# Causal attention with its probabilities built with keys on partitions: maxima from a separate pass, shift and sums as products with ones, two heads on the halves of the array

## The chip, the cores and the metric

The kernel runs on 1 core of one Trainium2 chip. The metric is device time in microseconds (us). The kernel before takes 1363.31 us, the median of 3 runs (1360.38 to 1364.28).

## The reference

The program is four layers on `x` of shape (1, 2048, 128): causal softmax attention with 16 heads of 64, a gated feed-forward layer, a linear attention, and the feed-forward layer again. Only the first is changed:

```python
K = jnp.einsum('bpd,ihd->biph', x, W_K)
Q = jnp.einsum('bpd,ihd->biph', x, W_Q)
V = jnp.einsum('bpd,ihd->biph', x, W_V)
scores = jnp.einsum('biph,biqh->biqp', K, Q)
scores = jnp.where(mask[None, None, :, :], scores, NEG_INF)
attn = jax.nn.softmax(scores / np.sqrt(d_head).astype(np.float32), axis=-1)
z = jnp.einsum('biph,biqp->biqh', V, attn)
out = jnp.einsum('bqf,df->bqd', z_flat, W_O)
```

`x` in it is the normalised input, and `out` is added to the residual. Everything is fp32.

## The kernel before, in words

`attention` (L192) handles the 16 heads as 8 pairs. The 2048 positions are 16 tiles of 128, and 4 chunks of 512. A pair's steps `j` = 0 to 7 are two tiles of queries each, so a step has four rows of work `u` (2 tiles by 2 heads). For each row and each chunk of keys up to the diagonal:

- **Scores** (L516 to L519). Queries stand on the partitions. Q is split into a rounded part and a remainder (`q_hi`, `q_lo`), K likewise, and K's two parts of 64 rows are stacked into 128 (`k_st`), so two matmuls over all 128 rows give all four products. Matmuls of type fp32r are used. At the diagonal a bf16 matmul adds the mask (L518). The scores lie in a ring of 5 PSUM banks.
- **Softmax.** VectorE takes the negated maximum of each row and chunk (L353); ScalarE computes the exponentials into `prob` in SBUF with this as bias, and sums them along the way (L434, with an ACTIVATION_READ_ACCUMULATOR for the sum). Small instructions (L306 to L369) combine chunks, and each piece of `prob` is multiplied by its factor: three in four on GpSimd (L325), one in four on VectorE (L382).
- **Turning.** The value product needs keys on partitions, so each 128x128 block of `prob` is transposed by TensorE (L530) and copied to `probT` by ScalarE (L448) for one head and VectorE (L376) for the other.
- **Values** (L545): fp32 matmuls with 64 columns of V as weights, each head to its own half of the output partitions; then a copy (L455), the output projection (L555) and the addition to `x` (L391).

Each pair's K and Q come from L561, V from L568. ScalarE writes the rounded parts (L464, L466), VectorE the remainders (L408, L410), and SP copies `q_parts` to the other 64 partitions by DMA (L287). fp32 matmuls show in the trace as two records of two streams each.

The order of every engine's work is made by `attention_plan` (L51), a list scheduler over assumed durations; it emits one list per engine. Each engine then runs its list in order, and waits on semaphores. `fetch` (L1211) loads the feed-forward weights and clears its scratch rows; SP issues it once the first pair's projections are through.

## Time and profile before

| | |
|---|---|
| median of 3 runs | 1363.31 us |
| profiled execution | 1360.53 us, span 1358.8 us |
| mean granted TensorE clock | 0.944 |
| PE busy | 1173.5 us, 86% |
| DVE, ACT, POOL busy | 957.3, 794.6, 829.2 us |
| attention, from the page's stretches and the timeline | up to about 1018 us |

The profile's page gives busy time per engine and a strip of 40 equal slices; the trace gives windows, groups of instructions by line, the waits and a timeline. PE is the matmul row, PEld the row of weight loads, DVE is VectorE, ACT ScalarE, POOL GpSimd. The duration of a matmul record includes the time until its result has left the array, so what a matmul costs in a stream is read from one start to the next. All times below are of the one profiled execution.

### The profile page before, as it was taken

The page shows a single profiled execution, that of the slowest core. Times are in us where ns is not written, and L with a number is a line of the kernel's source. Part 1 is how long each engine was busy: PE and PEld are TensorE (multiplying, and loading weights), DVE is VectorE, ACT ScalarE, POOL GpSimd, SP SyncE. Part 2 cuts the span into 40 slices and gives each one's busy share as a digit, 9 for nine tenths or more (in the row PEclk, how much of TensorE's full clock was granted, in tenths as well). Part 3 has the DMA queues.
Part 4 walks back from the last instruction along what each step waited for, and adds up shares of the span by engine and source line. Part 5 has one row for each costly group of instructions (what it writes and reads, how often), then busy time and mean ns, then how long its engine had stood idle before and what let it go on. Part 6 is the DMA issues. An engine that isn't in the chain of part 4 may idle for free. (4 is left out here: it accounts for less than half of the span.)

```text
span 1358.8 us, 24424 instructions
## 1 busy us (share of the span) xinstructions
PE 1173.5 (86%) x7936; PEld 855.3 (63%) x7936; DVE 957.3 (70%) x2108; ACT 794.6 (58%) x2192; POOL 829.2 (61%) x813
## 2 busy tenths in 40 slices
PE   5999999999999999999999999999973585885285
PEld 4666667676767767676676667676753582443285
DVE  5878677867776786878677777867743355998254
ACT  6777576767757775766677576766721342322053
POOL 0675668757866775887576768757852443552433
PEclk9899999999999999999999999999995796998588
DMA  4950200200020011002000200200000221000023
GB/s 124 125 141 16 48 1 1 52 12 1 1 63 1 1 32 32 1 1 63 1 1 8 57 1 1 50 14 1 1 1 17 57 61 32 1 0 1 29 60 98
DMA packets 52689, 41.18 MB, mean 30 GB/s; under 512 B 14177, under 2 KB 41442, under 8 KB 52578
## 3 DMA queue, kind: packets, MB, share of 16 engines
q1 hardware_dynamic: 50018, 34.50, 11.9%
q0 software_dynamic: 2560, 5.26, 1.2%
q8 instruction: 62, 1.02, 0.3%
q14 instruction: 49, 0.40, 0.1%
HBM read 13.49 MB, written 9.48 MB: 17 GB/s over the span
## 5 line engine op out<-in xcount | busy, mean ns | idle before, releaser
L325 POOL TENSOR_SCALAR at_prob<-at_prob,at_scale 128x512 f32<-128x512 f32 (+1 forms) x480 | 656.2, 1383 | 5.6
L353 DVE TENSOR_REDUCE at_nmax<-at_ps 128x1 f32<-128x512 f32 (+3 forms) x640 | 375.9, 603 | 154.1 <-PE at_ps L519 150.5
L434 ACT ACTIVATE at_prob<-at_ps,at_nmax 128x512 f32<-128x512 f32 (+3 forms) x640 | 393.1, 623 | 44.6 <-DVE at_nmax L353 43.7
L530 PE MATMUL at_ps<-ident,at_prob 128*128 128x128 f32 x2176 | 328.7, 275 | 23.4 <-DVE at_probT L376 19.1
L530 PEld LDWEIGHTS at_ps<-ident,at_prob 128*128 128x128 f32 x2176 | 255.7, 140 | 110.5 <-issue 52.6
L516 PE MATMUL at_ps<-at_k_st,at_q_parts 128*128 128x512 f32 (+3 forms) x640 | 285.1, 445 | 6.1 <-ACT at_prob L434 3.6
L448 ACT ACTIVATE at_probT<-at_ps 128x512 f32<-128x512 f32 (+1 forms) x288 | 165.1, 573 | 212.2 <-PE at_ps L530 188.0
L545 PE MATMUL at_ps<-at_probT,at_v 128*64 128x256 f32 (+1 forms) x2304 | 270.1, 374 | 12.3 <-DVE at_probT L376 12.3
L519 PE MATMUL at_ps<-at_k_st,at_q_parts 128*128 128x512 f32 (+3 forms) x640 | 253.1, 396 | 0.0
L376 DVE COPY at_probT<-at_ps 128x512 f32<-128x512 f32 (+1 forms) x288 | 189.0, 656 | 68.1 <-PE at_ps L530 64.7
L545 PEld LDWEIGHTS at_ps<-at_probT,at_v 128*64 128x64 f32 x2304 | 155.2, 136 | 107.1 <-issue 48.5
L516 PEld LDWEIGHTS at_ps<-at_k_st,at_q_parts 128*128 128x128 f32 x640 | 122.2, 191 | 46.7 <-ACT at_prob L434 22.0
L434 ACT ACTIVATION_READ_ACCUMULATOR at_prob<-at_ps,at_nmax 128x1 f32 x640 | 131.1, 205 | 0.0
L519 PEld LDWEIGHTS at_ps<-at_k_st,at_q_parts 128*128 128x128 f32 x640 | 125.8, 197 | 1.3
L382 DVE TENSOR_SCALAR at_prob<-at_prob,at_scale 128x512 f32<-128x512 f32 (+1 forms) x160 | 93.0, 583 | 2.5 <-POOL at_scale L318 2.0
L727 POOL DMA_INDIRECT slots_out<-f_ys,f_back x48 | 47.2, 984 | 63.9 <-DVE f_ys L836 49.2
L866 ACT ACTIVATE f_hT<-f_ps,f_wfix 128x128 f32<-128x128 f32 x192 | 54.6, 370 | 34.1 <-PE f_ps L911 28.8
L306 POOL TENSOR_TENSOR at_gap<-at_low,at_nmax 128x8 f32<-128x8 f32 (+2 forms) x48 | 9.9, 206 | 93.8 <-DVE at_low L358 93.8
L720 POOL DMA_INDIRECT slots_in<-f_xn,f_pos_u x32 | 31.3, 980 | 55.7 <-DVE f_pos_u L811 46.6
L904 PE MATMUL f_ps<-ident,f_xs 128*128 128x128 f32 x48 | 14.2, 296 | 57.3 <-DMA f_xs<-slots_in 57.3
L1037 POOL TENSOR_TENSOR li_outer<-li_qk,li_v 128x1152 f32<-128x1152 f32 x16 | 35.5, 2220 | 44.1 <-DVE li_qk L1063 44.1
L316 POOL COPY at_scale<-at_rinv 128x4 f32<-128x4 f32 x16 | 3.0, 189 | 96.6 <-DVE at_rinv L364 96.6
(189 smaller groups left out, 1364.1 us busy)
## 6 DMA issues: line engine op xcount, KB each, us to landing
at_q_parts<-at_q_parts SPq DMA_DIRECT2D x64, 256.0 KB, 3.5
f_xs<-slots_in SPq DMA_DIRECT2D x48, 64.5 KB
slots_in<-zeros SPq DMA_DIRECT2D x2, 1536.0 KB, 19.4
wall<-in_L_ffn_w_dram SPq DMA_DIRECT2D x1, 2048.0 KB, 19.8
wall<-in_L_ffn_w_dram SPq DMA_DIRECT2D x4, 512.0 KB, 6.1
f_got<-slots_out SPq DMA_DIRECT2D x8, 256.0 KB, 3.6
out_dram<-x SPq DMA_DIRECT2D x4, 256.0 KB, 2.4
slots_out<-f_ys,f_back POOLq DMA_INDIRECT x48
```

The costliest lines, as they stand in the source:

```text
L325: pool.tensor_scalar(cols, cols, scale[:, k, u, c:c + 1], None, ALU.mult).then_inc(s_fix["pool"], 1)
L353: dve.tensor_reduce(nmax[:, j % 2, u % 4, c:c + 1], bank, AX.X, ALU.max, negate=True).then_inc(s_max, 1)
L376: dve.tensor_copy(probT[1][n % TURNED][:, 0:w], turn_ps[1][:, 0:w]).then_inc(s_probT[1], 1)
L382: dve.tensor_scalar(cols, cols, scale[:, k, u, c:c + 1], None, ALU.mult).then_inc(s_fix["dve"], 1)
L434: act.activation(prob[j % 2][u % 4][:, c * BANK:c * BANK + w], ring[use_of["score", p, u, c] % RING][:, 0:w], ACT.Exp, bias=nmax[:, j % 2, ...
L448: act.activation(probT[0][n % TURNED][:, 0:w], turn_ps[0][:, 0:w], ACT.Copy).then_inc(s_probT[0], 1)
L516: pe.matmul(bank[:, 0:w], q_hi[h][:, r * P:(r + 1) * P], keys, start=True, stop=False)
L519: pe.matmul(bank[:, 0:w], q_lo[h][:, r * P:(r + 1) * P], keys, start=False, stop=True).then_inc(s_score, 1)
L530: last = pe.transpose(turn_ps[h][:, b * P:(b + 1) * P], prob[j % 2][2 * i + h][:, t * P:(t + 1) * P], ident[:, :])
L545: last = pe.matmul(z_ps[part_of, to:to + w], v[:, t, part_of], probT[h][group(p, j, g) % TURNED][:, 2 * P * b:2 * P * b + w], start=t == 0 ...
L727: pool.indirect_dma_start(scratch_out[:, :], bass.IndirectOffsetOnAxis(ap=back[k][:, :], axis=0), ys[k][:, :], None).then_inc(s_store[k], 16)
L866: last = act.activation(hT[k][:, f, :], ps[2 + c % 2][:, f * P:(f + 1) * P], ACT.Gelu, bias=wfix[k][:, B1.start + f:B1.start + f + 1])
```

## The change

The softmax is computed in another layout. `attention_order` replaces `attention_plan`: a fixed order with constants instead of durations. Work now goes by chunks of 512 queries (4 per pair), and by tiles of 128 keys inside them (4, 8, 12 and 16 tiles). A pair has 40 such tiles, and 40 items of the separate maxima pass.

- **Maxima pass** (`peakscore`): for 128 queries and up to 512 keys, one product `q_hi` by `k_hi` per head over 64 rows; at the diagonal four matmuls add the mask. VectorE takes maxima over both heads at once (`max`), and the smallest negated one (`peak`), which matmuls with the identity turn into a row (`turn`), copied to `shift`.
- **Scores** (`score`): keys on partitions, 512 queries as columns. Four products per head over 64 rows, the heads on the upper and lower half of the array and in two banks, plus one matmul with ones that adds `shift`. At the diagonal only the columns that count are computed.
- ScalarE takes the exponential of both heads (up to 128x1024) straight into `probT`, without bias and sum. GpSimd zeroes the masked triangle (`select`).
- **Values** as before, per tile with up to 512 columns. The **sums** of the probabilities are matmuls with 32 columns of ones, on the quarters of the output partitions.
- **End of a chunk**: copies (`leave`), a matmul that spreads the sums (`spread`), a VectorE reciprocal of 128x512 (`share`), a GpSimd product (`divide`), then the output projection.
- The PSUM ring is 3 pairs of banks, shared by all items but the values. `probT` has 6 buffers. The copies by DMA are gone; `fetch` is issued when the setup's transposes are done. GpSimd prepares more constants, and the setup's transposes wait for them.

```diff
-RING = 5
-TURNED = 4
+WAITING = 6
+RUN = 2
+AHEAD = 20
...
+    RING = 3
...
-                for _, p, c in order["sp"]:
...
+                sp.wait_ge(s_setT, N_SET)
+                fetch(sp)
...
+                    if kind == "select":
...
+                        pool.affine_select(out=tile, in_=tile, compare_op=ALU.is_ge, fill=0.0, base=0,
+                                           pattern=[[0, 2], [1, P]], channel_multiplier=-1).then_inc(s_select, 1)
+                    else:
...
+                        pool.tensor_tensor(z_sb[g % 2][:, :], z_sb[g % 2][:, :], share[:, :], ALU.mult).then_inc(s_zn, 1)
...
+                        dve.tensor_reduce(nmax[:, g % 2, t, :, k], ring[use_of["peakscore", p, c, t, k] % RING][:, :, 0:w], AX.X, ALU.max,
+                                          negate=True).then_inc(s_max, 1)
...
+                        dve.reciprocal(share[:, :], ring[use_of["spread", p, c] % RING][:, 0, :]).then_inc(s_share, 1)
...
+                        act.activation(probT[n % WAITING][:, :, at:BANK], ring[use_of["score", p, c, t] % RING][:, :, at:BANK],
+                                       ACT.Exp).then_inc(s_exp, 1)
...
-                pe.wait_ge(s_const, 3)
+                pe.wait_ge(s_const, CONSTS)
...
+                        for h in range(2):
+                            last = pe.matmul(banks[:, h, 0:w], q_hi[p % 2][head(h), (TPC * c + t) * P:(TPC * c + t + 1) * P],
+                                             k_hi[p % 2][head(h), k * BANK:k * BANK + w], start=True, stop=k < c)
+                        if k == c:
+                            for i in range(2):
+                                for h in range(2):
+                                    last = pe.matmul(banks[:, h, w - P:w], pick[i][head(h), :], mask[i][head(h), :], start=False, stop=i == 1)
...
+                        for a, b in ((k_hi, q_hi), (k_hi, q_lo), (k_lo, q_hi), (k_lo, q_lo)):
+                            for h in range(2):
+                                pe.matmul(banks[:, h, at:BANK], a[p % 2][head(h), keys], b[p % 2][head(h), queries], start=a is k_hi and b is q_hi, stop=False)
+                        for h in range(2):
+                            last = pe.matmul(banks[:, h, at:BANK], onesr[head(h), :], shift[c][head(h), at:BANK], start=False, stop=True)
...
+                        for t in tiles:
+                            at = skipped(c, t)
+                            for h in range(2):
+                                r = h + 2 * (t % 2 if c else 0)
+                                last = pe.matmul(l_ps[32 * r:32 * r + 32, at:BANK], ones[:, :], probT[tile_no[p, c, t] % WAITING][:, h, at:BANK],
+                                                 start=t == 0 or (t == 1 and c > 0), stop=t >= TPC * (c + 1) - (2 if c else 1))
```

What TensorE runs in the middle of a pair before (scores by L516 and L519, transposes by L530, values by L545):

```order
L545 MATMUL at_ps<-at_probT,at_v 64x256 [waits at_s_probT0,at_s_probT1,at_s_zT,at_s_v]
L545 MATMUL at_ps<-at_probT,at_v 64x256 x7
L516 MATMUL at_ps<-at_k_st,at_q_parts 128x512 [waits at_s_exp]
L519 MATMUL at_ps<-at_k_st,at_q_parts 128x512
L530 MATMUL at_ps<-ident,at_prob 128x128 [waits at_s_probT1,at_s_fix_dve,at_s_fix_pool]
L530 MATMUL at_ps<-ident,at_prob 128x128 x3
L516 MATMUL at_ps<-at_k_st,at_q_parts 128x256 [waits at_s_exp]
L518 MATMUL at_ps<-at_maskb,at_identb 128x128
L519 MATMUL at_ps<-at_k_st,at_q_parts 128x256
L530 MATMUL at_ps<-ident,at_prob 128x128 [waits at_s_probT0,at_s_fix_pool]
L530 MATMUL at_ps<-ident,at_prob 128x128 x3
```

And in the middle of a pair after the change (L454 and L459 the maxima pass, L475 and L477 the scores and the shift, L491 the values, L497 the sums, L503 the spread of the sums, L507 the output projection; line numbers are the changed kernel's):

```order
L507 MATMUL at_ring<-at_wo,at_z_sb 128x128 [waits at_s_zn,at_s_exp]
L507 MATMUL at_ring<-at_wo,at_z_sb 128x128 x3
L503 MATMUL at_ring<-at_l_sb,at_gather 128x512 [waits at_s_l,at_s_max]
L491 MATMUL at_z<-at_probT,at_v 64x512 [waits at_s_z,at_s_v,at_s_exp]
L491 MATMUL at_z<-at_probT,at_v 64x512 x3
L497 MATMUL at_l<-at_probT,at_ones 32x512 x4
L454 MATMUL at_ring<-at_k_hi,at_q_hi 128x128 [waits at_s_hi,at_s_exp]
L454 MATMUL at_ring<-at_k_hi,at_q_hi 128x128
L459 MATMUL at_ring<-at_mask,at_pick 128x128 x4
L475 MATMUL at_ring<-at_q_hi,at_k_hi 128x512 [waits at_s_shift,at_s_lo,at_s_add]
L475 MATMUL at_ring<-at_q_hi,at_k_hi 128x512
L475 MATMUL at_ring<-at_q_lo,at_k_hi 128x512 x2
```

The transposes are gone, each tile of scores has ten matmuls (two behind each of five weights), and every item waits for the reader of the item three before it (`at_s_max`, `at_s_exp`, `at_s_add`) instead of five.

On VectorE the maxima of the next chunks stand behind the reciprocal and the remainders:

```order
L323 TENSOR_REDUCE at_nmax<-at_ring 128x2 [waits at_s_peakscore] x3
L336 TENSOR_TENSOR at_k_lo<-at_ring,at_k_hi 128x512 [waits at_s_hi]
L337 SCALAR_TENSOR_TENSOR at_q_lo<-at_ring,at_q_hi 128x512
L343 RECIPROCAL at_share<-at_ring 128x512 [waits at_s_zn,at_s_spread]
L323 TENSOR_REDUCE at_nmax<-at_ring 128x2 [waits at_s_peakscore] x4
L350 TENSOR_TENSOR x<-at_ring,x 128x512 [waits at_s_add,at_s_o]
```

The list before had a copy of transposed probabilities or a scaling between every two or three maxima; these are gone.

## Rows read from the trace of the kernel before

**Rows 1.** The page: busy time, and 40 slices of the span

```profile
PE 1173.5 (86%) x7936; PEld 855.3 (63%) x7936; DVE 957.3 (70%) x2108; ACT 794.6 (58%) x2192; POOL 829.2 (61%) x813
PE   5999999999999999999999999999973585885285
```

**Rows 2.** Two of four windows of one pair each: busy us (instructions), clock, DMA

```profile
140.00:262.00 122.00, 116.88 (x827) 84.41 (x824) 90.50 (x178) 83.64 (x227) 84.73 (x80) 1.00 0.07 16
...
506.00:628.00 122.00, 117.75 (x833) 85.36 (x832) 92.70 (x180) 84.93 (x231) 85.64 (x80) 1.00 0.08 18
```

**Rows 3.** Groups by line, shapes kept apart: busy, mean ns | idle before

```profile
L325 POOL TENSOR_SCALAR at_prob<-at_prob,at_scale 128x512 f32<-128x512 f32 x320 | 511.7, 1613 | 4.7
L434 ACT ACTIVATE at_prob<-at_ps,at_nmax 128x512 f32<-128x512 f32 x448 | 304.7, 687 | 22.7 <-DVE at_nmax L353 21.9
L353 DVE TENSOR_REDUCE at_nmax<-at_ps 128x1 f32<-128x512 f32 x448 | 299.4, 684 | 125.4 <-PE at_ps L519 123.6
...
L325 POOL TENSOR_SCALAR at_prob<-at_prob,at_scale 128x128 f32<-128x128 f32 x64 | 38.3, 599 | 0.1
...
L408 DVE TENSOR_TENSOR at_k_st<-at_ps,at_k_st 64x512 fp32r<-64x512 f32 x64 | 44.1, 689 | 8.5 <-ACT at_k_st L464 6.9
...
L464 ACT ACTIVATE at_k_st<-at_ps 64x512 fp32r<-64x512 f32 x64 | 37.7, 589 | 11.4 <-PE at_ps L561 10.9
...
L434 ACT ACTIVATE at_prob<-at_ps,at_nmax 128x128 f32<-128x128 f32 x64 | 23.5, 367 | 14.2 <-DVE at_nmax L353 14.1
...
L353 DVE TENSOR_REDUCE at_nmax<-at_ps 128x1 f32<-128x128 f32 x64 | 18.0, 282 | 13.7 <-PE at_ps L519 13.5
```

**Rows 4.** Timeline of PE, fp32r scores in a row, then four transposes

```profile
609.03 0.40 PE L516 MATMUL at_ps<-at_k_st,at_q_parts 128*128 128x512 f32 x1
609.27 0.40 PE L519 MATMUL at_ps<-at_k_st,at_q_parts 128*128 128x512 f32 x1
609.50 0.60 PE L530 MATMUL at_ps<-ident,at_prob 128*128 128x128 f32 x4
609.86 0.48 PE L516 MATMUL at_ps<-at_k_st,at_q_parts 128*128 128x512 f32 x1
```

**Rows 5.** Timeline of PE, a packed run of values, eight matmuls

```profile
1009.38 1.95 PE L545 MATMUL at_ps<-at_probT,at_v 128*64 128x256 f32 x16
1011.26 0.98 PE L530 MATMUL at_ps<-ident,at_prob 128*128 128x128 f32 x7
```

**Rows 6.** Timeline of PE, an unpacked fp32 projection, eight records of L568

```profile
26.34 1.02 PE L561 MATMUL at_ps<-at_xnT,at_wT_k 128*128 128x512 f32 x2
27.20 1.05 PE L568 MATMUL at_ps<-at_wT_v,at_xnT 128*128 128x128 f32 x8
28.10 0.59 PE L561 MATMUL at_ps<-at_xnT,at_wT_q 128*128 128x512 f32 x1
```

**Rows 7.** Timeline of PEld: loads of 128 columns, gate product (clock at half)

```profile
1029.68 1.83 PEld L890 LDWEIGHTS f_ps<-f_gate,f_xnT 128*128 128x128 f32 x8
```

**Rows 8.** Timeline of PE: a score of 128 columns with its mask

```profile
42.16 0.22 PE L516 MATMUL at_ps<-at_k_st,at_q_parts 128*128 128x128 f32 x1
42.23 0.23 PE L518 MATMUL at_ps<-at_maskb,at_identb 128*128 128x128 bf16 x1
42.26 0.31 PE L519 MATMUL at_ps<-at_k_st,at_q_parts 128*128 128x128 f32 x1
42.41 0.52 PE L530 MATMUL at_ps<-ident,at_prob 128*128 128x128 f32 x3
```

**Rows 9.** Groups: reciprocals of 4 and of 16 elements

```profile
L364 DVE RECIPROCAL at_rinv<-at_esum 128x4 f32<-128x4 f32 x16 | 2.7, 170 | 0.7 <-ACT at_prob L434 0.7
...
L1073 DVE RECIPROCAL li_den<-li_den 128x16 f32<-128x16 f32 x16 | 4.0, 252 | 0.6
```

**Rows 10.** Timeline: the setup's constants on POOL, first transposes

```profile
4.51 0.29 POOL L298 TENSOR_SCALAR_AFFINE_SELECT at_maskb<-at_maskb 128x128 bf16<-128x128 bf16 x1
...
11.54 4.58 PE L487 MATMUL at_ps<-ident,at_prob 128*128 128x128 f32 x24 [11.54 <-DMA at_prob<-in_L_attn_a_W_Q_dram]
```

More of the change, by code:

```diff
@@ L195, in attention @@
     SCALE = float(DH) ** -0.5
-    STEPS = NT // 2
-    order, row, chunks, width, turned, fixer, run_of = attention_plan(PAIRS, NT, NC, TPC)
-    uses = [it for it in order["pe"] if it[0] in ("score", "project", "vproject", "out")]
+    order, runs = attention_order(PAIRS, NC, TPC)
+    RING = 3
+    uses = [it for it in order["pe"] if it[0] != "value"]
     use_of = {it: n for n, it in enumerate(uses)}
@@ L207, in attention, with head, cols, skipped @@
             count_of[(e,) + it] = ran[it[0]]
-    def group(p, j, g):
-        return p * STEPS * (STEPS + 1) // 2 + j * (j + 1) // 2 + g
-    value_run = {}
-    for it in order["pe"]:
-        if it[0] == "value":
-            for g in run_of(it[2], it[3]):
-                value_run[group(it[1], it[2], g)] = count_of[("pe",) + it]
+    tile_no, run_of = {}, {}
+    for i, run in enumerate(runs):
+        for n, it in enumerate(run):
+            tile_no[it], run_of[it] = RUN * i + n, run[0]
+    tile_at = {n: it for it, n in tile_no.items()}
+    def head(h):
+        return slice(DH * h, DH * (h + 1))
+    def cols(c):
+        return slice(c * BANK, (c + 1) * BANK)
+    def skipped(c, t):
+        return max(t - TPC * c, 0) * P
     with ExitStack() as ctx:
@@ L258, in attention @@
+        mask = [sb(f"mask{i}", [P, P], F32R) for i in range(2)]
+        onesr = sb("onesr", [P, P], F32R)
+        ones = sb("ones", [P, 32])
+        gather = sb("gather", [P, P])
+        draft = [probT[0][:, 0, i * P:(i + 1) * P] for i in range(4)] + [probT[1][:, 0, i * P:(i + 1) * P] for i in range(3)]
         s_xin, s_win = sem("s_xin"), [sem(f"s_win{i}") for i in range(4)]
[L259 removed]
+        s_c0, s_draft, s_halves, s_const = sem("s_c0"), sem("s_draft"), sem("s_halves"), sem("s_const")
@@ L391, in _ @@
+                        rows = x[:, TPC * c:TPC * (c + 1), :]
+                        o = ring[use_of["out", p, c] % RING][:, 0, :]
                         dve.tensor_tensor(rows, o.rearrange("p (t d) -> p t d", d=D), rows, ALU.add).then_inc(s_add, 1)
                         if p == PAIRS - 1:
-                            dve.wait_ge(s_add, q + 1)
-                            for t in (2 * j, 2 * j + 1):
+                            dve.wait_ge(s_add, g + 1)
+                            for t in range(TPC * c, TPC * (c + 1)):
@@ L554, in _ @@
-                        for i in range(2):
-                            last = pe.matmul(ring[use_of[it] % RING][:, i * D:(i + 1) * D], zT[q % 2][:, i * P:(i + 1) * P], wo[:, p, :],
-                                             start=True, stop=True)
+                        pe.wait_ge(s_zn, g + 1)
+                        for t in range(TPC):
+                            last = pe.matmul(banks[:, 0, t * P:(t + 1) * P], z_sb[g % 2][:, t * P:(t + 1) * P], wo[:, p, :], start=True, stop=True)
                         last.then_inc(s_o, 1)
@@ L558, in _ @@
                     elif kind == "project":
-                        _, _, c, i = it
-                        free_bank(it)
-                        pe.matmul(ring[use_of[it] % RING][:, :], wT["kq"[i]][:, p, :], xnT[:, c * BANK:(c + 1) * BANK],
-                                  start=True, stop=True).then_inc(s_proj, 1)
+                        for i, n in enumerate("kq"):
+                            last = pe.matmul(banks[:, i, :], wT[n][:, p, :], xnT[:, cols(c)], start=True, stop=True)
+                        last.then_inc(s_proj, 1)
```

591 lines of the change are left out of this document (249 added, 342 removed).

## The prediction

> **What bounds the kernel now.** I read the page first. TensorE is busy for 86% of the span and at nine tenths or more in all slices from about 34 to 1000 us [rows 1]: attention is one long stretch in which TensorE is the bound, and what follows it is not touched. Then the windows of a pair. I chose 122 us, and two of the four windows have nearly the same counts [rows 2]: PE is busy 116.9 to 117.8 of 122 us at a granted clock of 1.00, VectorE 90 to 93, ScalarE and GpSimd about 85. So one pair costs 122 us, 8 pairs cost 976, and a change is worth what it does to TensorE's 122 us, unless it makes another engine later than that. VectorE's idle time of 123.6 us before the maxima is a wait for scores [rows 3], so it follows and does not lead.
>
> Then I looked for prices in a stream, from start to start. All durations are of one profiled execution, 1360.53 us, 0.2% under the median of 1363.31; the sum is made against 1360.5. One measurement of this kernel can tell 0.3%, some 4 us, from no change.
>
> - An fp32r matmul of 512 columns takes 0.24 and 0.23 us [rows 4]: 0.235.
> - An fp32 matmul of 512 columns on the whole array takes 0.86 us, and one of 128 columns 0.90/4 = 0.225 [rows 6].
> - Eight value matmuls of 256 columns, on alternating halves of the columns, take 1.88 us [rows 5]. Alone each would take 0.43, together 3.44. Two at a time give 1.72, and 0.16 us is left for going into and out of the tiled array: 0.08 per change of tiling. A packed pair of 512 columns costs 0.86.
> - Loads of 4-byte weights, 128 columns: at half the clock eight take 1.83 us, the last of them 0.33, so one starts each 0.214 us [rows 7], and 0.107 at the full clock. With scores of 128 columns, two such loads and one bf16 mask cover 0.25 us from L516 to the next transpose [rows 8], which agrees: short matmuls cost their loads.
>
> **The change, part by part, for one pair.** A full item counts as 512 columns; the causal triangle is 34 of these per head (28 full, and 4 each of 384, 256 and 128).
>
> (1) Removed: 272 transposes. Four start 0.36 us apart from the next score [rows 4], and delay its second half by about 0.1: near 0.11 each, 30 us. The copies, the scaling on GpSimd (1.61 us a piece, [rows 3]) and the chain of small instructions were beside TensorE; their loss gives nothing by itself. The scores (128 full-width slots for two heads, and the narrow ones) were some 33 us.
>
> (2) Scores. Two heads on the two halves, so ten matmuls are five slots if halves overlap. No row of before shows halves of the rows at work at once. Its cost lies between the packed slot, 0.86/4 = 0.215 per 512 fp32r columns (the value rows, halves of the columns), and the unpacked double, 0.47. I take the fp32r row, 0.235, and full overlap, since the nearest packed rows lose nothing. 28 full items: 28 x 5 x 0.235 = 32.9. The 12 narrow ones are bound by ten loads, 1.07 us each, 12.8 (five slots of 384 columns are only 0.88). Sum 45.7.
>
> The loads are where the trace is silent: it has none of 64 rows. It could be half as long or go on beside the other half's load, 0.054 effective, or be 0.107 one behind the other. I take 0.107, as in rows 7; at 0.054 narrow scores and masks would save 10 us a pair. The Trainium skill (TensorE: Matmul & The Clock Gate, LDWEIGHTS) says that a load's time is its columns and that fewer rows take as long; it speaks against the change, and by it the saving of 10 is out.
>
> (3) Maxima pass. 24 full items at 0.235 = 5.6. The 16 diagonal ones have six loads each (two products, four mask matmuls), 0.64 us, 10.3. Sum 15.9. Nothing of this existed before but 32 masks of 0.04 us [rows 8].
>
> (4) Values: 34 packed pairs x 0.86 = 29.2, before nearly the same.
>
> (5) Sums: 68 fp32 matmuls with 32 columns. The first chunk uses two quarters (2.5 slots x 0.86 = 2.2); the others have 31.5 slots on four quarters, 0.43 if four work at once, 13.5. Sum 15.7. If only two do, 29.2.
>
> (6) Per pair also: turning the maxima, 16 loads, 1.7; spreading the sums, 4 x 0.86 = 3.4. Projections (6.9), V (32 records of 0.112, 3.6) and output (3.6) stay, 14.1.
>
> (7) Changes of tiling: three for each of 20 runs of values and sums, two for each of 20 items that use the whole array: 100 x 0.08 = 8.0 (before some 40 x 0.08).
>
> Sum: 45.7 + 15.9 + 29.2 + 15.7 + 5.1 + 14.1 + 8.0 = 133.7 us of TensorE.
>
> (8) Waits. Other engines per pair, from rows 3: a maximum costs 0.684 at 512 columns and 1.05 ns per column more, so 1.22 at 1024; all maxima are 42, with remainders (8 x 0.69), additions and reciprocals some 66. A reciprocal goes from 170 to 252 ns for 12 elements more [rows 9], 6.8 ns each: 3.6 us for 512. Exponentials: 0.83 ns per column, 1.11 at 1024, 39 in all, ScalarE 54. GpSimd under 25. None reaches 134. But the ring is three deep. A projection's banks are held for two copies and two subtractions, 2 x 0.589 + 2 x 0.689 = 2.6 us [rows 3], while the two items behind it give 1.4 to 2.4; 4 of these and 4 spreads held for 3.6 us are each worth about 1 us. A score frees its banks after 1.11 us and handing over, against 1.4 us of a maximum and a score: about nothing to 0.2. Between 3 and 12 us a pair; I take 7 (before: 122 less 117.7 busy, 4.3).
>
> (9) Start. GpSimd makes some 27 constants before TensorE may start: 8 fills of about 0.2 and 5 selects of 0.29 [rows 10], two copies of 512 columns (1.61 each) and ten smaller ones (0.6, both by GpSimd's nearest rows [rows 3]), some 13 us from 3.6 us on. The transposes began at 11.54 [rows 10] and then waited for weights: +5 us. `fetch` moves ahead and the 64 copies by DMA vanish; attention reads none of `fetch`'s data and copies of later pairs were issued long before use: 0. The last chunk ends through copies, reciprocal, product and output, some 10 us, where before the last scalings and transposes ran with TensorE half idle: 0.
>
> A pair: 133.7 + 7 = 140.7 against 122, +18.7; eight pairs +150, and 5: **1360.5 + 155 = 1516 us**, 11% slower. The same prices give the kernel before 33 + 1.3 + 30 + 29.2 + 14.1 + 3.2 = 111 and 4.3 idle, 115 of its 122 us; the other 7 are small delays where kinds of matmuls meet. The new stream has fewer such places beyond those counted in (7), so I don't add them, but were they there again, it would be +56.
>
> **The rivals.**
> Packing pays less than full. If quarters work only two at a time: +13.5 x 8 = 108, 1624. Against it, the values lose nothing on two halves [rows 5]; there is no row for four. The Trainium skill (same page, Part 3) measured 3.07 times for four row tiles. As a mechanism here, with a loss like this, each half slot of scores and maxima would be 30% longer, (32.9 + 5.6) x 0.3 x 8 = +92, 1608.
>
> Halves of the rows don't overlap: scores double but stay over their loads, 28 x 10 x 0.235 = 65.8 and 12 narrow ones 16.3, +36; maxima +7; less waiting, -3: +40 a pair, 1836. Against it: halves of the columns do overlap. For it: no row.
>
> The readers are late: ring waits of 17 us a pair rather than 7, 1596. For it: three places rather than five, the 3.6 us reciprocal with four maxima behind it. Against: every other engine has half its time free.
>
> The other side: the parts of the array are fully independent, also in loading weights and in changing the tiling. Then narrow scores fall to 8.0 (-4.8), diagonal maxima by 5.1, tiling by 8.0, slots to 0.215 (-3.3): -21.2, a pair of 119.5, 1360.5 - 20 + 5 = 1346, and 1290 if the waits go too. It decides once a pair is under 121.4 us. Against it: 0.16 us around each run of values [rows 5].
>
> **How the numbers follow.** Forecast 0.51 (its own range 1455 to 1580, from slots of 0.215 to 0.235, waits of 3 to 12, and those 56); packing less than full 0.20; late readers 0.10; no overlap of halves 0.12; other side 0.07. The range 1440 to 1640 takes in the first three, 0.81. Faster by over 0.3%: 0.06; within 0.3%: 0.02, at the edge of the other side; slower 0.92.
>
> **What would show it.** Right: PE over 90% busy at clock 1.00, a score item of 512 columns starting its ten matmuls within 1.1 to 1.2 us, in pairs a tenth apart; diagonal maxima items at 0.64; four sums of 512 columns in 0.9 us; attention ending near 1173. Wrong: matmuls of the two heads one behind the other by 0.2 us, four sums in 1.7 us, PE idle before maxima or scores with VectorE or ScalarE named for over 15 us a pair, or narrow scores of 128 columns under 0.6 us.

## The result and the profile after

The changed kernel takes 1478.2 us (median of 4, 1477.4 to 1480.4) where the kernel before takes 1361.85 (median of 4): 1.0856 times as long, 95% interval 1.0832 to 1.0881. The profiled execution took 1480.4 us, its span is 1478.7. The forecast was 1516, its range 1440 to 1640: slower, as predicted, and 38 us less slow.

The page of the changed kernel, busy time and two lines of its slices:

```profile
PE 1290.6 (87%) x9024; PEld 739.9 (50%) x9024; DVE 724.9 (49%) x1148; ACT 501.8 (34%) x864; POOL 240.7 (16%) x359
...
PE   5899999999999999999999999999996295886376
...
PEclk9999999999999999999999999999998587899588
```

Against [rows 1], VectorE has lost 232 us of work, ScalarE 293 and GpSimd 589, and TensorE has gained 117. The stretch at nine tenths now lasts to about 1110 us instead of 1000: all the engines that were relieved had stood beside the one that got more to do.

The window of one pair, from its first projection to that of the next pair; the three before and behind are the same within 0.01 us (us and instructions of each engine, the granted clock last but two):

```profile
503.87:641.24 137.37, 132.27 (x970) 70.52 (x969) 64.14 (x61) 48.68 (x64) 11.66 (x20) 1.00 0.00 1
```

A pair takes 137.4 us where it took 122.4 (the same measure on the kernel before; [rows 2] used 122). 8 x 15.0 = 120 us, and the spans differ by 1478.7 - 1358.8 = 119.9: the pairs hold the whole loss, the start and the layers behind attention hold none.

Groups by line, shapes kept apart (busy, mean ns | idle before, and what ended it), for [rows 3] and [rows 9]:

```profile
L323 DVE TENSOR_REDUCE at_nmax<-at_ring 128x2 f32<-128x1024 f32 x224 | 272.7, 1225 | 351.0 <-PE at_ring L454 286.9 <-PE at_ring L459 64.0
...
L343 DVE RECIPROCAL at_share<-at_ring 128x512 f32<-128x512 f32 x32 | 107.4, 3357 | 65.7 <-PE at_ring L503 65.7
...
L475 PEld LDWEIGHTS at_ring<-at_q_lo,at_k_hi 64*128 64x128 f32 x640 | 60.6, 186 | 5.8
```

The maximum of 1024 columns takes 1.225 us (1.22 was worked out from its shorter forms), the exponential 1.03 (1.11), the reciprocal 3.36 (3.6). Nearly all idle time of VectorE and ScalarE in attention is a wait for PE.

### The profile page after: what moved, and what is told of

The parts are those of the page before. It is cut to its first block and busy times, and to the rows that moved or that the text cites. A ratio compares the mean times of both kernels' runs of the same rounds, so it can differ in the third digit from the quotient of the medians.

```text
span 1478.7 us, 23229 instructions
## 1 busy us (share of the span) xinstructions
PE 1290.6 (87%) x9024; PEld 739.9 (50%) x9024; DVE 724.9 (49%) x1148; ACT 501.8 (34%) x864; POOL 240.7 (16%) x359
## 5 line engine op out<-in xcount | busy, mean ns | idle before, releaser
L323 DVE TENSOR_REDUCE at_nmax<-at_ring 128x2 f32<-128x1024 f32 (+2 forms) x320 | 338.5, 1065 | 490.6 <-PE at_ring L454 286.9
L381 ACT ACTIVATE at_probT<-at_ring 128x1024 f32<-128x1024 f32 (+1 forms) x320 | 286.5, 897 | 649.7 <-PE at_ring L477 648.4
L491 PE MATMUL at_z<-at_probT,at_v 128*64 128x512 f32 (+3 forms) x1280 | 270.4, 543 | 0.0
L497 PE MATMUL at_l<-at_probT,at_ones 128*32 128x512 f32 (+3 forms) x1280 | 162.9, 540 | 0.0
L454 PE MATMUL at_ring<-at_k_hi,at_q_hi 64*128 64x512 f32 (+3 forms) x640 | 135.4, 422 | 7.8 <-DVE at_q_lo L337 4.0
L491 PEld LDWEIGHTS at_z<-at_probT,at_v 128*64 128x64 f32 x1280 | 77.8, 136 | 124.4 <-issue 98.0
L475 PE MATMUL at_ring<-at_q_hi,at_k_hi 64*128 64x512 f32 (+3 forms) x640 | 129.2, 400 | 7.8 <-DVE at_nmax L323 7.6
L454 PEld LDWEIGHTS at_ring<-at_k_hi,at_q_hi 64*128 64x128 f32 x640 | 59.8, 185 | 147.8 <-issue 119.4
L475 PE MATMUL at_ring<-at_q_lo,at_k_hi 64*128 64x512 f32 (+3 forms) x640 | 116.9, 362 | 0.0
L475 PE MATMUL at_ring<-at_q_hi,at_k_lo 64*128 64x512 f32 (+3 forms) x640 | 116.9, 361 | 0.0
L475 PE MATMUL at_ring<-at_q_lo,at_k_lo 64*128 64x512 f32 (+3 forms) x640 | 116.9, 361 | 0.0
L477 PE MATMUL at_ring<-at_shift,at_onesr 64*128 64x512 f32 (+3 forms) x640 | 116.5, 360 | 0.0
L497 PEld LDWEIGHTS at_l<-at_probT,at_ones 128*32 128x32 f32 x1280 | 28.7, 108 | 109.5 <-issue 107.9
L475 PEld LDWEIGHTS at_ring<-at_q_hi,at_k_hi 64*128 64x128 f32 x640 | 60.4, 185 | 35.2 <-DVE at_nmax L323 24.9
L477 PEld LDWEIGHTS at_ring<-at_shift,at_onesr 64*128 64x128 f32 x640 | 60.5, 185 | 9.7
L475 PEld LDWEIGHTS at_ring<-at_q_lo,at_k_lo 64*128 64x128 f32 x640 | 60.3, 185 | 9.8
L475 PEld LDWEIGHTS at_ring<-at_q_hi,at_k_lo 64*128 64x128 f32 x640 | 60.3, 185 | 9.7
L475 PEld LDWEIGHTS at_ring<-at_q_lo,at_k_hi 64*128 64x128 f32 x640 | 60.6, 186 | 5.8
```

The lines of the kernel that those rows point to most:

```text
L323: dve.tensor_reduce(nmax[:, g % 2, t, :, k], ring[use_of["peakscore", p, c, t, k] % RING][:, :, 0:w], AX.X, ALU.max, negate=True).then_inc ...
L381: act.activation(probT[n % WAITING][:, :, at:BANK], ring[use_of["score", p, c, t] % RING][:, :, at:BANK], ACT.Exp).then_inc(s_exp, 1)
L454: last = pe.matmul(banks[:, h, 0:w], q_hi[p % 2][head(h), (TPC * c + t) * P:(TPC * c + t + 1) * P], k_hi[p % 2][head(h), k * BANK:k * BANK ...
L475: pe.matmul(banks[:, h, at:BANK], a[p % 2][head(h), keys], b[p % 2][head(h), queries], start=a is k_hi and b is q_hi, stop=False)
L477: last = pe.matmul(banks[:, h, at:BANK], onesr[head(h), :], shift[c][head(h), at:BANK], start=False, stop=True)
L491: pe.matmul(z_ps[head(h), at:BANK], v[p % 2][:, t, head(h)], probT[tile_no[p, c, t] % WAITING][:, h, at:BANK], start=t == 0, stop=t == TPC ...
```

## Where the 137.4 us of a pair go

Timeline of PE in the changed kernel, a full diagonal item of the maxima pass, a full tile of scores, and the next item ("x2" are the two heads):

```profile
608.73 0.50 PE L454 MATMUL at_ring<-at_k_hi,at_q_hi 64*128 64x512 f32 x2
609.07 0.34 PE L459 MATMUL at_ring<-at_mask,at_pick 64*128 64x128 f32 x4
609.24 0.45 PE L475 MATMUL at_ring<-at_q_hi,at_k_hi 64*128 64x512 f32 x2
609.52 0.40 PE L475 MATMUL at_ring<-at_q_lo,at_k_hi 64*128 64x512 f32 x2
609.76 0.40 PE L475 MATMUL at_ring<-at_q_hi,at_k_lo 64*128 64x512 f32 x2
609.99 0.40 PE L475 MATMUL at_ring<-at_q_lo,at_k_lo 64*128 64x512 f32 x2
610.23 0.39 PE L477 MATMUL at_ring<-at_shift,at_onesr 64*128 64x512 f32 x2
610.45 0.40 PE L454 MATMUL at_ring<-at_k_hi,at_q_hi 64*128 64x512 f32 x2
```

Both heads together start a product each 0.23 us: the halves of the rows overlap in full. A full score item takes 1.21 us (1.1 to 1.2 predicted). The full diagonal maxima item takes 0.51, not 0.64, and the narrower ones 0.37 to 0.40. The reason stands in the view of the loads for the same moment:

```profile
609.18 0.19 PEld L475 LDWEIGHTS at_ring<-at_q_hi,at_k_hi 64*128 64x128 f32 x2
609.29 0.19 PEld L475 LDWEIGHTS at_ring<-at_q_lo,at_k_hi 64*128 64x128 f32 x2
```

Two loads, one for each half, start together (0.003 to 0.004 us apart in the records) and are over in 0.19; the next two follow 0.11 later. I had taken 0.107 for each, one behind the other. Narrow tiles of scores show it best (timeline of PE, a tile of 256 and one of 128 columns):

```profile
602.20 0.28 PE L475 MATMUL at_ring<-at_q_hi,at_k_hi 64*128 64x256 f32 x2
...
602.80 0.39 PE L454 MATMUL at_ring<-at_k_hi,at_q_hi 64*128 64x512 f32 x2
603.69 0.33 PE L475 MATMUL at_ring<-at_q_hi,at_k_hi 64*128 64x128 f32 x2 [0.50 <-DVE at_nmax L323]
603.85 0.27 PE L475 MATMUL at_ring<-at_q_lo,at_k_hi 64*128 64x128 f32 x2
...
604.19 0.28 PE L477 MATMUL at_ring<-at_shift,at_onesr 64*128 64x128 f32 x2
604.40 1.12 PE L503 MATMUL at_ring<-at_l_sb,at_gather 128*128 128x512 f32 x2
```

The five slots of the 256-column tile take 0.60 us, where 1.07 was predicted. Those of the 128-column tile take 0.71 here, with a wait in front and an fp32 matmul behind: the first slot 0.16, the last 0.21, and the three between 0.11 to 0.12 each. Over five pairs tiles of 128 columns take 0.60 to 0.71. And the values and sums (timeline of PE, one run of two key tiles):

```profile
1090.60 1.94 PE L491 MATMUL at_z<-at_probT,at_v 128*64 128x512 f32 x8
1092.46 1.07 PE L497 MATMUL at_l<-at_probT,at_ones 128*32 128x512 f32 x8
1093.46 0.50 PE L475 MATMUL at_ring<-at_q_hi,at_k_hi 64*128 64x512 f32 x2
```

Each fp32 matmul has two records, so x8 are four matmuls. Four values take 1.86 us, two at a time. Four sums take 1.00 us, four at a time. Changing over is in both: by the prices of the prediction the streams alone are 1.72 and 0.86. The first fp32r product behind such work takes 0.33 us instead of 0.23, as at 608.73 above (0.34).

From start to start over five pairs (251.6 to 938.5 us of the trace), the parts of a pair add up as follows; a run is the values and sums of two key tiles, 20 a pair. The predicted column gives each part its changes of tiling at the 0.08 of term 7.

| part of a pair | predicted | measured |
|---|---|---|
| scores with shift: 28 full, 4 of 384, 8 narrower | 45.7 | 42.4 |
| maxima pass (L454 12.1, L459 3.0) | 15.9 | 15.1 |
| values and sums (32.2 + 19.0) | 44.9 + 4.8 | 51.2 |
| turning, spread, projections, V, output | 19.2 + 3.2 | 22.6 |
| waits and changes behind scores | 7 | 6.1 |
| pair | 140.7 | 137.4 |

The scores are 28 x 1.20 + 4 x 0.97 + 8 x 0.61 from timelines, without what stands behind them. From their first start to the next item's they take 48.5 us a pair, and the row of waits and changes is what is left of that. PE's idle time alone is 137.37 - 132.27 = 5.1 us a pair.

The same count in the kernel before, in us a pair: scores with masks 44.5, transposes 32.0, values 32.4, projections, V and output 13.5, in all 122.4. So the transposes went, and the sums (19.0), the maxima pass (15.1), the spread (4.2), the turning (2.3) and a longer score part (+4.0) came.

The longest rows of PE's own waits in attention, in the changed kernel (us in total, times, longest):

```profile
PE at_ring L503 <- DVE at_q_lo L337: 19.0, 14, 1.4
...
PE at_ring L507 <- DVE at_q_lo L337: 9.7, 7, 1.4
PE at_ring L475 <- DVE at_nmax L323: 7.6, 15, 0.6
```

The first two are the projections' banks, held for two copies and two subtractions: with 4.0 us before the maxima they make 32.7 us, 4.1 a pair. The third is a wait for maxima, which term 8 did not name. The reciprocal, which it did, is not among them.

## The experiments

Each time is a median of 4 runs. The kernel before, timed beside them, took 1360.8, 1360.7, 1359.6 and 1360.3 us. Differences to the changed kernel are taken from ratios times 1360, and are uncertain by some 4 us.

| kernel | us | ratio to before, 95% | against the change |
|---|---|---|---|
| heads_apart | 1489.9 | 1.0938 (1.0920 to 1.0956) | +11 |
| two_quarters | 1584.1 | 1.1628 (1.1609 to 1.1648) | +105 |
| recip_copy | 1476.2 | 1.0843 (1.0825 to 1.0861) | -2 |
| no_mask | 1458.3 | 1.0725 (1.0707 to 1.0743) | -18 |
| no_swap | 1469.1 | 1.0808 (1.0786 to 1.0830) | -7 |
| run4 | 1601.6 | 1.1786 (1.1764 to 1.1809) | +126 |
| run4_copy | 1473.1 | 1.0835 (1.0812 to 1.0858) | -3 |
| joined | 1334.8 | 0.9804 (0.9788 to 0.9821) | -143 |
| joined_nm | 1326.3 | 0.9748 (0.9728 to 0.9768) | -151 |
| joined_nmns | 1345.8 | 0.9896 (0.9874 to 0.9917) | -131 |
| joined_hi | 1253.8 | 0.9232 (0.9208 to 0.9256) | -221 |
| hi_nmns | 1264.5 | 0.9302 (0.9280 to 0.9324) | -211 |

### Do the halves need their matmuls in turns: heads_apart

```
-for a, b in ((k_hi, q_hi), (k_hi, q_lo), (k_lo, q_hi), (k_lo, q_lo)):
-    for h in range(2):
+for h in range(2):
+    for a, b in ((k_hi, q_hi), (k_hi, q_lo), (k_lo, q_hi), (k_lo, q_lo)):
```

> Scores only: the four products of head 0 are issued in a row, then the four of head 1, then the two matmuls with ones. Same work. If the halves of the array have queues of their own deep enough, nothing changes: 1478 +-8. If each half can hold only one waiting matmul, head 1 begins two slots late: two slots of 0.233 us more on each of 28 full tiles and about half of that on the narrow ones, some 15 us a pair, about 1600. If matmuls start strictly in order and only neighbours on different halves overlap, 8 products take 7 slots instead of 4: some 22 us a pair, about 1655.

Measured: 1489.9 us, +11. The four products of one head are issued before those of the other, and still run beside them. Timeline of PE in this kernel:

```profile
602.90 0.50 PE L475 MATMUL at_ring<-at_q_hi,at_k_hi 64*128 64x512 f32 x2
603.13 0.50 PE L475 MATMUL at_ring<-at_q_lo,at_k_hi 64*128 64x512 f32 x2
```

Each pair of equal products still starts in one slot of 0.23 us; by the names in these records the second head's first product starts before the first head's second, though three others stand between them in the program. So products queued for a busy half do not hold up the other half. Both rivals fall, one waiting matmul a half (about 1600) and overlap of neighbours alone (about 1655), by the time itself. The order is not free, though: +11 is outside the 8 us expected. In the records the two heads now start up to 0.11 us apart, not 0.003, and a pair takes 138.5 us for 137.4, all of the difference in the starts behind L477 (15.7 us a pair for 14.6).

### Do four quarters work at once: two_quarters

```
-r = h + 2 * (t % 2 if c else 0)
+r = h
```

> The sums use two quarters of the columns in every chunk (as they did only in the first), not four. If four quarters work at once in the changed kernel, each run of sums doubles from 0.86 to 1.72 us: +13.5 us a pair, 1478 + 108 = 1586. If four quarters were already served two at a time: 1478.

Measured: +105 us, as expected of quarters that do work at once (1586 expected, 1584 measured). Timeline of PE in this kernel, the same run of eight records as above with two quarters:

```profile
603.82 1.94 PE L491 MATMUL at_z<-at_probT,at_v 128*64 128x512 f32 x8
605.68 1.91 PE L497 MATMUL at_l<-at_probT,at_ones 128*32 128x512 f32 x8
607.52 0.39 PE L454 MATMUL at_ring<-at_k_hi,at_q_hi 64*128 64x256 f32 x2
```

Four sums of 512 columns take 1.84 us from start to start on two quarters and 1.0 on four. The term of 13.5 against 27 us a pair stands, and with it the price of the sums: even on four quarters they cost TensorE 19 us a pair for numbers that the kernel before got beside its exponentials.

### Does the reciprocal hold the ring: recip_copy

```
-dve.reciprocal(share[:, :], ring[use_of["spread", p, c] % RING][:, 0, :])
+dve.tensor_copy(share[:, :], ring[use_of["spread", p, c] % RING][:, 0, :])
```

The division by the sums is left out.

> The reciprocal of 128x512 (3.36 us) becomes a copy (about 0.69 us); this leaves out the division. VectorE loses 85 us of work. If TensorE's stream is the bound and the ring's waits come from the projection's banks: 0 to -8 us, 1470 to 1478. If late readers, the reciprocal first, make the waits: -30 us or more, under 1450.

Measured: -2 us, whose interval overlaps that of the change. Here the 3.36 us of the reciprocal are hidden by the items that stand between it and the next use of its bank. The reciprocal as a late reader falls, for this order of the work; run4 shows how close it was.

### What the maxima's masks cost: no_mask

The lines of L459 are left out, so that a shift may be larger than the row's true maximum; the score tiles keep their mask.

> The two mask products a head of the maxima pass are left out (32 places, two matmuls per head, 128 columns), so the maxima may include keys behind the diagonal: the shift is then at least the true maximum, and the probabilities and their sums come out of it in the same proportion. The mask itself stays in the scores made with keys on partitions. In the trace of the changed kernel those products take 3.0 us from start to start a pair of heads. If TensorE alone sets the time: 8 x 3.0 = 24 us less, about 1454 us. If the pair is set by the chain maximum -> peak -> turn -> shift, in which these products stand too, also about that; if a wait takes their place (VectorE's maxima, 24.9 us of TensorE's waits in all), 1465 to 1478.

Measured: -18 us of 24 by the ratios, -20 by the medians. In the trace a pair falls by 2.5 us of the 3.0 left out, since the starts of the maxima's own products now take 13.1 us and not 12.1: part of the time that the masks had stood for is still spent there. TensorE's loads waited for the maxima 35.6 us in all and not 24.9, but PE's own wait for them before the scores stayed at 7.6, so that the rest turned into waits is not shown.

```profile
PEld at_ring L471 <- DVE at_nmax L323: 35.6, 80, 0.9
```

### The projections' banks: no_swap

```
-for i in range(len(dve) - 2, -1, -1):
-    if dve[i][0] == "low" and dve[i + 1][0] == "max":
-        dve[i], dve[i + 1] = dve[i + 1], dve[i]
```

> VectorE's subtraction that empties a bank of a projection is no longer put behind the next maximum (1.22 us). In the changed kernel TensorE waits on this subtraction 49 us in all (25.0 and 12.6 and 11.6 by its rows at the spread, the output product and the maxima). If those waits are what is left of the ring's stalls: 10 to 30 us less, 1450 to 1468. If the maximum that comes later then is itself waited for (24.9 us already), nothing changes: 1472 to 1484. If it is worse: up to 32 x 1.2 / 2 = 19 us more, 1497.

Measured: -7 us by the ratios, -9 by the medians, and in the trace 1.4 us a pair, 11 in eight: about the low end of what was expected. The waits that it shortens are those for the projections' banks (12.7 us before the spread for 19.0, and 6.5 before the output product for 9.7):

```profile
PE at_ring L500 <- DVE at_q_lo L334: 12.7, 14, 0.9
```

### The changes of tiling: run4 and run4_copy

```
-RUN = 2
-WAITING = 6
+RUN = 4
+WAITING = 8
```

(with V in one buffer and the setup's tiles in another place, to make room)

> The value products and sums of a unit are taken in runs of four key tiles and not of two, eight probability tiles wait and not six (the setup's transients lie elsewhere, V has one buffer), so that there are about 15 fewer runs a pair, each of which enters and leaves the tiling of the values and of the sums. Theory (a change of tiling costs 0.095 us from start to start, and the first fp32r product behind it 0.10 more): 15 runs x (2 x 0.095 + 0.10) is 4 us a pair, so 1446 us, in a range of 1440 to 1455. Rival (a change is free and what stands between the runs is a wait for exp): 1470 to 1480. With V in one buffer and four tiles to wait for before a run, a wait could also take over: over 1485.

Measured: +126 us, outside everything expected. The window of one pair (columns as above) and the timeline of PE show why:

```profile
274.50:428.00 153.50, 138.41 (x968) 78.25 (x968) 63.09 (x60) 48.75 (x64) 11.55 (x20) 0.94 0.00 1
```

```profile
610.54 0.39 PE L480 MATMUL at_ring<-at_shift,at_onesr 64*128 64x512 f32 x2
612.69 0.51 PE L457 MATMUL at_ring<-at_k_hi,at_q_hi 64*128 64x512 f32 x2 [1.76 <-DVE at_share L344]
613.23 0.54 PE L478 MATMUL at_ring<-at_q_hi,at_k_hi 64*128 64x512 f32 x2
613.58 0.62 PE L478 MATMUL at_ring<-at_q_lo,at_k_hi 64*128 64x512 f32 x2
614.00 0.63 PE L478 MATMUL at_ring<-at_q_hi,at_k_lo 64*128 64x512 f32 x2
```

With four tiles in a run there is less between the spread and the item that wants its bank, and TensorE waits 1.76 us for the reciprocal. Behind the wait the same products start each 0.42 us instead of 0.23: 512 columns at 1.2 GHz, the lower level. In the windows of this stretch the granted clock is 1.00 in the wait, then 0.60, 0.75, and 1.00 again:

```profile
611.00:613.00 2.00, 0.31 (x2) 0.19 (x2) 2.00 (x2) 0.99 (x1) 0.28 (x1) 1.00 0.00 0
613.00:616.00 3.00, 2.96 (x14) 1.58 (x14) 1.41 (x2) 0.48 (x1) 0.99 (x1) 0.60 0.02 5
616.00:618.00 2.00, 2.00 (x10) 0.57 (x8) 0.00 (x0) 0.54 (x1) 0.00 (x0) 0.75 0.00 0
618.00:620.00 2.00, 2.00 (x14) 0.52 (x14) 0.00 (x0) 0.00 (x0) 0.00 (x0) 1.00 0.00 0
```

Such a wait thus costs about as much again in the 5 us behind it: 3 x 0.4 + 2 x 0.25 = 1.7 us of lost clock. There are 29 of them in eight pairs. A pair grew by 16.1 us (153.5 against 137.4): PE's idle time from 5.1 to 15.1, 6.4 of it for the reciprocal, and by an estimate 0.06 x 153.5 = 9 us of lost clock, less some 3 for ten runs fewer. To take the reciprocal out and leave the rest:

> run4 with the reciprocal replaced by a copy of the same bank (the division by the sums is left out, POOL multiplies by the sums). In run4 TensorE stood 1.8 us, 29 times, for a bank that the reciprocal (3.36 us) still read, and behind such a wait the granted clock fell (0.94 over five pairs, fp32r products 0.42 us instead of 0.23). If that is what ate run4's gain: the pair is 137.4 less 4 us for the 10 places fewer a pair at which values follow sums and maxima, and less the waits on the reciprocal, so 1440 to 1455 us. If longer runs or V in one buffer cost something by themselves: 1500 to 1590.

Measured: 1473.1, so the reciprocal and what hangs on it was worth 128 us in this order. The rival of 1500 or more, that longer runs or one V buffer cost that much by themselves, falls; but only 3 of the 30 us expected of fewer changes came, and against recip_copy, which also leaves out the division, the difference is within the noise. They were there and were given back. From start to start over five pairs, values and sums together fell from 255.9 us (recip_copy) to 241.8, 14.1 us for 50 runs fewer: **0.28 us for one run**, in the rows of values and sums alone. What a run costs the fp32r products around it stands in their rows: the first one behind it takes 0.335 us instead of 0.23, and a last score product in front of values 0.32. Scores, shift and maxima even so rose by 16 us in the same five pairs and the spreads fell by 5; what rose is mostly a wait in front of the maxima that comes to 4.0 us in the changed kernel and to this here:

```profile
PE at_ring L457 <- DVE at_q_lo L338: 18.1, 10, 2.0
```

### Sums and values in one product: joined

The rows above ask for a kernel without tiling in the values. The probabilities are made as fp32r, so they are rounded, which the kernels before and after the change don't do. V is split into two fp32r parts by one more subtraction, and its weights are `[V of head 0 | 64 ones | V of head 1]`. One product of 128 columns of weights then gives 64 rows of values and, in the other 64, the sums, already spread: the sums, their spread by `gather` and the column tiling of values and sums go. To make room, `probT` has 4 buffers instead of 6 and V one set instead of two, and the reciprocal reads a copy in SBUF and no bank of the ring.

```
-for h in range(2):
-    pe.matmul(z_ps[head(h), at:BANK], v[p % 2][:, t, head(h)], probT[...][:, h, at:BANK], ...)
-for h in range(2):
-    pe.matmul(l_ps[32 * r:32 * r + 32, at:BANK], ones[:, :], probT[...][:, h, at:BANK], ...)
+for part in (v_hi, v_lo):
+    for h in range(2):
+        pe.matmul((z_ps, l_ps)[h][:, at:BANK], part[:, t, DH * h:DH * h + P], probT[...][:, h, at:BANK], ...)
```

> Values and sums as one product on the whole array: probabilities written as fp32r, V split into a rounded part and a remainder, each head's weights 64 columns of V beside 64 columns of ones (zeros with the remainder). Values and sums cost 51.2 us a pair in the changed kernel's trace; four fp32r matmuls per tile cost 28 x 4 x 0.235 + 6.6 = 33, with about 3 for entering. The spread of the sums goes (4.2 and some waits). If TensorE's time is the sum of its matmuls by type: -19 to -25 us a pair, 1280 to 1330, below the kernel before. If the ring's waits or the readers take over, less than half of it: 1400 or more.

Measured: 1334.8 us, 0.980 of the kernel before: faster than both kernels, 5 us above the 1280 to 1330 that was expected. Timeline of PE, one key tile (four products), and a window of a pair:

```profile
501.58 0.39 PE L508 MATMUL at_z<-at_probT,at_v_hi 128*128 128x512 f32 x1
501.81 0.40 PE L508 MATMUL at_l<-at_probT,at_v_hi 128*128 128x512 f32 x1
502.04 0.39 PE L508 MATMUL at_z<-at_probT,at_v_lo 128*128 128x512 f32 x1
502.27 0.39 PE L508 MATMUL at_l<-at_probT,at_v_lo 128*128 128x512 f32 x1
```

```profile
227.80:346.70 118.90, 112.07 (x800) 81.80 (x800) 65.52 (x64) 53.75 (x72) 11.55 (x20) 1.00 0.00 1
```

A key tile costs 0.92 us where values and sums cost 1.86/2 + 1.00/2 = 1.43. By the same rows four fp32r products are no cheaper than two packed fp32 values (0.92 and 0.93), so the gain is the sums and their changes; no run has fp32r values with the sums kept apart. Over five pairs L508 takes 179.5 us against 255.9, 15.3 less a pair, and the spread's 4.2 go: 19.5 of gain, and 18.5 came. PE's idle time grew from 5.1 to 6.8 us a pair, as the wait for the maxima before the scores grew (7.6 us in PE in the changed kernel, 34.7 here):

```profile
PEld at_ring L491 <- DVE at_nmax L332: 62.4, 74, 1.8
...
PE at_ring L491 <- DVE at_nmax L332: 34.7, 43, 1.4
```

> As joined (values and sums of a head as one product on the whole array, V in two fp32r parts with ones beside it), with the products of V's lower part left out: it prices these. They are 72 full products or 0.2 us each a pair: 13.6 tiles' worth of 512 columns, 2 heads, at 0.23 us a product plus narrow ones, about 16 us a pair or 125 us in all. If TensorE sets the time: 1335 - 125 = 1210 us. If the ring and VectorE's maxima and exp hold it (in joined TensorE already waited 97 us for VectorE at the value products), much less is gained: 1260 to 1310.

This one has `for part in (v_hi,):`, so V counts in one fp32r part. Measured: 1253.8 us, 81 less than joined and not 125. The products left out were 179.5 / 2 / 5 = 18 us a pair, and the pair fell from 118.9 to 109.1: that is just over half of them. PE's idle time grew from 6.8 to 10.9 us a pair, mostly by waits for VectorE's maxima (54.5 us by the row of PE, 34.7 in joined), and the granted clock over its pairs is 0.98, for 1.00 in joined.

> joined with the maxima's mask products left out (the maxima may include keys behind the diagonal) and VectorE's subtractions in their own order. no_mask was worth 20 us and no_swap 9 us on the changed kernel; both also shorten what VectorE's maxima wait for. If they add up: 1335 - 29 = 1306 us. If VectorE's maxima hold the ring in joined (97 us of waits at the value products), less: 1315 to 1330. Above 1335 would mean that the order of VectorE's subtractions helps there.

> As joined_nmns, with the products of V's lower part left out too, so that V counts in fp32r's precision alone. Joined_hi less 29 us is 1225; if waits for the maxima and a lower clock take part of it, 1230 to 1250.

They have the edits of no_mask and no_swap on top of joined and of joined_hi. Measured: 1345.8 and 1264.5, each 11 us *slower* than without the two. The expectation that gains add up was wrong in both.

> joined with the maxima's mask products left out, and VectorE's subtractions behind the next maximum as in joined: of the two edits of joined_nmns (1346 us, 11 over joined) only the first. If the order of the subtractions was what made that kernel slower, this one gains the mask products (15 us a pair's worth over five pairs, 3.0 a pair, 24 in all, less what turns into waits for maxima): 1312 to 1328 us. If leaving out the mask products itself turns into waits (VectorE's maxima hold the ring): 1333 to 1346.

Measured: 1326.3, 8.5 us faster than joined and 19.5 faster than joined_nmns. So the order of VectorE's subtractions, worth -7 us in the changed kernel, costs some 20 here: in joined TensorE waits for the maxima, and an order that puts the subtraction first makes them late. The waits at the scores, first of joined_nm, then of joined_nmns:

```profile
PEld at_ring L487 <- DVE at_nmax L332: 78.9, 102, 2.1
```

```profile
PEld at_ring L484 <- DVE at_nmax L329: 91.3, 102, 2.7
```

From 350 to 600 us the granted clock is 1.00 in the first and 0.98 in the second. PE's idle time grew by 1.2 us a pair, 9 in eight. The rest goes with the clock: its mean over the whole run fell from 0.931 to 0.921, by an estimate 0.01 x 1340 = 13 us. joined_nm is the fastest version that keeps V in both parts.

## Why the prediction held, point by point

**What bounds it** was right: a pair is TensorE's, and 1114 us of relief on three other engines came to nothing.

**Term 2, scores: 45.7, measured 42.4.** The full items were right (1.18 taken, 1.20 measured), and the assumption that the halves of the rows overlap, for which there was no row, held. The size of the narrow items was wrong: 12.8 taken, 8.8 measured. The step that failed, though the total held, is "I take 0.107, as in rows 7": it prices each load one behind the other, and the loads of two halves go side by side. The other end that the same paragraph named, 0.054 effective, is what ran. It saves 4.0 us in the narrow scores and 3.7 in the 16 diagonal maxima items (10.3 taken, 6.6 measured), of the 10 named. The Trainium skill (TensorE: Matmul & The Clock Gate, LDWEIGHTS) says that fewer rows load no faster. This trace agrees for one load: 0.19 us for 64 rows, where the scores of before (L516, L519) have 0.19 to 0.20 for 128. But the rule is about one load, and my sentence that by it "the saving of 10 is out" went further than it does. By Part 3 of the same page of the Trainium skill a load overlaps a matmul in flight only in another row group. The trace has more overlap than that: by the records the two loads of 609.29 start together, while the products of 609.24 are in flight on the same halves.

**Term 3, maxima pass: 15.9, measured 15.1.** The diagonal items were too dear by the same loads (10.3 against 6.6 us a pair), and the 24 others too cheap (5.6 against 8.5): half of them stand behind sums or projections and take 0.335 us, the other half, behind scores, 0.28 and waits. That the term came out within 1 us is luck, two errors of some 3 us with opposite signs.

**Terms 4, 5 and 7: 49.7, measured 51.2.** Two and four tiles of the array at once lose nothing beyond the changing over: four sums take 1.00 us, against 0.86 for their streams, and 1.84 on two quarters. A run's changes were put at 3 x 0.08 = 0.24, and its values and sums cost 0.28 more than their streams, by run4_copy and by the timeline (0.14 each). Not in the sum was the first fp32r product behind fp32 work, 0.33 us instead of 0.23. It was there to be read: in [rows 4] the score of 609.03 has its second product 0.24 later, and the score of 609.86, behind transposes, its mask's product only 0.31 later:

```profile
610.17 0.23 PE L518 MATMUL at_ps<-at_maskb,at_identb 128*128 128x128 bf16 x1
```

Term 1 had read this tenth as part of the price of transposes, and nothing charged it to the new stream. In the kernel before the first full product takes 0.32 us behind transposes, 175 times in seven pairs, and with the other places like it this comes to 4.0 us a pair of the 7 that the prediction left unexplained. The guess that the new stream has fewer such places was right, and the +56 did not come.

**Term 8, waits: 7, measured 5 to 6.** The projections' banks were put at about 1 us for each of 4 and cost 4.1 a pair. The 4 spreads, put at the same, cost nothing (recip_copy), and waits for maxima, not in the sum, cost 1.3. So the total is near for a reason that held only in half. VectorE's 66 us a pair were 64.1, ScalarE's 54 were 48.7, GpSimd's 25 were 11.7.

**Term 9, start: +5, measured 0.** The first projection starts at 20.30 us; in the kernel before it starts at 20.13. GpSimd's last constant is made at 10.8 and W_Q arrives at 11.4. The 13 us were too much, since I priced GpSimd's copies by its scalings: two of 512 columns took 1.17 us together, not 3.2, and ten small ones 0.29 each, not 0.6.

```profile
7.04 1.17 POOL L271 CAST at_peak<-at_probT 128x512 fp32r<-128x512 f32 x2
8.15 0.29 POOL L273 CAST at_identr<-ident 128x128 fp32r<-128x128 f32 x1
```

Together: 3.3 x 8 = 26 us for the pairs, 5 for the start, and 0.4 a pair because before takes 122.4: 155 - 26 - 5 - 3 = 121 of 120 measured.

**The rivals.** Quarters two at a time fell: two_quarters built that case and gave 1584 (1624 was the forecast plus 108; the difference is the forecast's own 38). Loss in row tiles, the other half of that rival, fell too: by the 3.07 times of the Trainium skill (same page, Part 3) each half slot would by an estimate have taken 0.30 us, and the trace has 0.23. Halves of the rows one after the other fell with the first timeline. Late readers fell, since PE's idle time is 5.1 us a pair and the reciprocal is worth 2 us in all (recip_copy), but not by much: run4 is this rival, with runs of four tiles. The other side was right in a part of its mechanism, the loads side by side, and wrong in the rest, since changing the tiling costs 0.28 a run.

**What would show it:** PE over 90% at clock 1.00 came as written (96%), and ten matmuls in 1.2 us nearly so, though the two of a slot start 0.003 us apart and not a tenth. Four sums took 1.00, not 0.9. Attention ended near 1135 us, not 1173, and the diagonal maxima took 0.51 or less. "Narrow scores of 128 columns under 0.6 us" was the sign of a wrong step: at 0.60 to 0.71 they stood on the line or above it, and that step was the wrong one.

## What to carry to other kernels

Work taken from engines that stand beside the bound is worth nothing, and what it costs the bound is worth all of it: here the sums, which had come beside the exponentials, and the maxima, which had been read from the scores themselves, became 34 us a pair of TensorE. Before tiling the array for a small product, ask whether it can be extra columns of a product that runs anyway; joined got the sums, already spread, for the 64 columns of weights that one head's V leaves free, and turned 9% slower into 2% faster, with rounded probabilities. A wait of nearly 2 us on TensorE cost about twice itself in run4, where the clock fell behind it, so an edit that lengthens a run or moves a subtraction is to be judged by the waits that it opens: one that gave 7 us in one kernel cost 20 in its neighbour.

## What was not expected of the hardware

- Loads of weights for the two halves of the rows run at the same time: two of 64 x 128 in 0.19 us, the next two 0.11 us behind. Two narrow fp32r products on halves, 128 or 256 columns, then take 0.11 to 0.12 us.
- The halves have work of their own waiting: with four products of one head standing ahead of the other's, both heads still ran in slots of 0.23 us (heads_apart).
- The first fp32r product of 512 columns behind fp32 or column-tiled work takes 0.32 to 0.34 us and not 0.23, in both kernels.
- An fp32r product on the whole array, 128 columns of weights, takes 0.23 us for 512 columns (joined), so values with V in two parts and the sums among them take 0.92 us a key tile, against 1.43 for tiled fp32 values and sums.
- After a wait of 1.76 us the granted clock was 0.60 and 0.75 in the next 5 us, with products of 512 columns each 0.42 us apart, and 1.00 again behind them (run4). Over five pairs the clock was 1.00 in the changed kernel, whose longest wait in PE there is 1.4 us, 1.00 in joined_nm with 1.6, and 0.98 in joined_hi and joined_nmns with 2.0 and 2.3.
- A reciprocal of 128x512 on VectorE takes 3.36 us, 2.7 times a maximum over 1024 columns.
